# Order of TensorE in a graph-network layer: the turns of the next tile ahead of layer 3 of an older one

## The reference, cut to what matters

```python
# x (12500, 128), dst (200000,) sorted, edge_attr_48 (200000, 48)
h = jnp.maximum(_layernorm(x, axis=-1), 0.0)
agg_edge = jax.ops.segment_sum(edge_attr_48, dst, num_segments=12500)
collected = jnp.concatenate([h, agg_edge], axis=1)        # 128 + 48 columns
a = jax.nn.silu(collected @ W1 + b1)                      # 256
b = jax.nn.silu(a @ W2 + b2)                              # 256
return x + (h + b @ W3 + b3)                              # 128
```

## Time and profile before

| what | value |
|---|---|
| median of 3 runs | 288.13 us |
| lowest and highest | 286.89 and 288.31 us |
| the profiled execution | 288.73 us |
| its span in the trace | 287.0 us |
| PE, DVE, ACT, POOL busy | 96%, 84%, 77%, 47% of the span |
| mean granted TensorE clock | 0.994 of full speed |

### The profile page before, as it was taken

The page is one execution under the profiler, slowest core; times in us unless marked ns, Lnnn a source line. Parts: engine busy times, 40 slices in busy tenths (PEclk is TensorE's granted clock), DMA queues, the critical chain, the costliest instruction groups (busy, mean ns, idle before and its releaser), DMA issues.

```text
span 287.0 us, 11959 instructions
## 1 busy us (share of the span) xinstructions
PE 274.2 (96%) x4286; PEld 248.4 (87%) x4287; DVE 241.2 (84%) x583; ACT 220.3 (77%) x424; POOL 135.7 (47%) x248
## 2 busy tenths in 40 slices
PE   7868999999999999999999999999999999999994
PEld 3756988999999999999999999999999999999793
DVE  7887998889898898998998889989898888986551
ACT  8856778787886888778877788787976878779662
POOL 4275565454455445454555446454455445452200
PEclk9979999999999999999999999999999999999999
DMA  6998965865688457865687547955687567820112
GB/s 168 323 306 249 204 171 147 248 187 166 170 251 246 142 158 221 256 178 162 182 246 218 173 137 240 256 168 162 187 251 224 149 170 227 253 82 21 30 38 62
DMA packets 79309, 53.28 MB, mean 186 GB/s; under 512 B 2984, under 2 KB 78850, under 8 KB 79288
## 3 DMA queue, kind: packets, MB, share of 16 engines
q1 hardware_dynamic: 79288, 53.04, 63.6%
HBM read 46.29 MB, written 6.40 MB: 184 GB/s over the span
## 4 chain that ended last, share of the span: by engine, by line
PE 85%; DVE 5%; issue 3%; ACT 3%; POOL 2%; ACTq 0%; POOLq 0%; DVEq 0%
PE agg_ps L1109 21%; PE z L1176 15%; PE z L1157 7%; PE z L1161 7%; PE z L1158 7%; PE agg_ps L1112 4%; PE z L1137 4%; PE tp L1123 4%; PE z L1143 4%; PE z L1142 3%; PE z L1139 3%; PE z L1138 3%; DVE onehot L786 2%; PE agg_ps L1040 1%; POOL agg_carry L498 1%
## 5 line engine op out<-in xcount | busy, mean ns | idle before, releaser
L498 POOL TENSOR_TENSOR agg_carry<-staged,agg_carry 48x42 f32 x196 | 92.8, 474 | 77.1 <-ACT staged L554 46.3
L1109 PEld LDWEIGHTS agg_ps<-onehot,raw 128*48 128x48 f32 x1560 | 73.6, 126 | 12.1 <-issue 12.1
L1109 PE MATMUL agg_ps<-onehot,raw 128*48 128x42 f32 x1560 | 77.0, 216 | 3.5 <-DVE onehot L786 3.5
L786 DVE TENSOR_TENSOR onehot<-window,rel 128x1176 f32<-128x1176 f32 (+1 forms) x57 | 77.5, 1363 | 0.5 <-ACT rel L546 0.5
L1112 PE MATMUL agg_ps<-onehot,raw 128*48 128x42 f32 x1568 | 77.2, 216 | 0.0
L1112 PEld LDWEIGHTS agg_ps<-onehot,raw 128*48 128x48 f32 x1568 | 73.9, 127 | 0.0
L479 POOL TENSOR_TENSOR rstd<-vareps,minus_half 128x4 f32<-128x4 f32 (+1 forms) x28 | 37.7, 1346 | 46.4 <-DVE vareps L771 46.4
L1176 PE MATMUL z<-w,h 128*128 128x128 f32 x392 | 51.2, 282 | 1.5 <-ACT h L625 1.1
L625 ACT ACTIVATE h<-z,b2c 128x448 f32<-128x448 f32 (+1 forms) x56 | 35.4, 633 | 19.5 <-PE z L1161 17.1
L1176 PEld LDWEIGHTS z<-w,h 128*128 128x128 f32 x392 | 46.0, 191 | 3.2 <-ACT z L621 1.4
L941 DVE TENSOR_TENSOR h_lo<-h,h_hi 128x448 fp32r<-128x448 f32 (+1 forms) x56 | 34.8, 624 | 12.1 <-ACT h_hi L639 7.6
(11 more groups left out here) (129 smaller groups left out, 411.9 us busy)
## 6 DMA issues: line engine op xcount, KB each, us to landing
raw<-in_edge_attr_dram SPq DMA_DIRECT2D x55, 672.0 KB, 5.9
x_t<-in_x_dram SPq DMA_DIRECT2D x14, 256.0 KB, 6.1
out_dram<-out_t SPq DMA_DIRECT2D x13, 256.0 KB
out_dram<-out_t SPq DMA_DIRECT2D x14, 192.0 KB, 6.0
x_t<-in_x_dram SPq DMA_DIRECT2D x13, 192.0 KB, 6.2
dst_rows<-in_dst_dram SPq DMA_DIRECT2D x1, 512.0 KB
agg_carry<-agg_carry SPq DMA_DIRECT2D x1, 336.0 KB, 8.0
raw<-in_edge_attr_dram SPq DMA_DIRECT2D x1, 288.0 KB, 3.6
```

The source lines that it names most:

```text
L498: pool.tensor_tensor(into, staged[:, parity, n, :], into, ALU.add).then_inc(s_added, 1)
L786: return dve.tensor_tensor(onehot[:, slot, at * PER:n * PER, :], window[:, :].unsqueeze(1).broadcast_to([P, cols_n, WINDOW]), cols.unsquee ...
L1109: mm = pe.matmul(banks[0:ED, bass.ds(offsets[at - first], WINDOW)], edges, into, start=False, stop=True, skip_group_check=True, tile_posit ...
```

## The change

In TensorE's list for a step the turns of tile i and layer 3 of tile i-2 change places. No instruction is added or taken away, no wait has another count, and the lists of the other engines stay as they are.

```diff
@@ -1189,10 +1189,10 @@
                     layer1(i - 1, 1 - parity)
                 if has(i, -1, NB):
                     sum_tile(i + 1, 1 - parity, offsets)
+                if has(i, 0, NT):
+                    transposes(i, parity)
                 if has(i, 2, NT):
                     layer3(i - 2, parity)
-                if has(i, 0, NT):
-                    transposes(i, parity)
                 if isinstance(i, int) and i == 1:
                     pe.wait_ge(s_w_lo, 3)
                     pe.wait_ge(s_w_hi, 4)
```

## The result

| | before | changed |
|---|---|---|
| median | 288.22 us (4 runs, 286.89 to 288.87) | 301.50 us (4 runs, 301.37 to 302.02) |
| profiled execution, its span | 288.73, 287.0 us | 301.37, 299.7 us |
| PE busy, share of the span | 96% | 91% |

The ratio is 1.047 with a 95% interval of 1.043 to 1.050: slower, by 13.3 us. The prediction had the sign and the place right and the size too large: it said 305.4, and its range began at 302.5. One run of all that follow, of the kernel with the early rows in the new order, took 335.97 us at a mean granted clock of 0.756, and the median given for that kernel is that of its nine other runs.

A forecast was written before the change was run, and what follows sets the result against it. The prediction took TensorE's list to bound the kernel; new waits for ScalarE's rows (7.2 + 9.5 + 0.2 + 0.4 = 17.3 us) on 288.73 gave 306.0, less 0.6 for the median: 305.4 us, range 302.5 to 309.

The forecast's parts named there:

- What bounds it, and what the change adds: TensorE, 85% of the last-ending chain, would newly wait for ScalarE's rows in 25 steps, mostly 0.50 or 0.76 us.
- VectorE wasn't pushed: Rival: layer 3 ends later than worked out and delays VectorE and the next sums; some 3 us, 308.4 us, chance 0.04.
- From ScalarE's end to TensorE's start: Handover from finished rows to TensorE's turns, taken as 0.10 us per step, nothing added for filling up again.
- Step 3: One of 12 odd steps: rows 0.49 us late by subtraction, priced at 0.50 + 0.10 us like the others.
- Step 26: Its stall of 0.86 us was to absorb TensorE's 0.43 wait in step 27, so it costs 0.4 us.
- The base of the sum: The 17.3 us were added to the profiled execution of 288.73 us; 0.6 us came off for the runs' median.
- The clock rival: New gaps of 0.6 to 0.9 us drop TensorE's clock in 25 steps; 45 us on top, 350 us, chance 0.03.
- The issue gap: Rival: a fifth of the 12.1 us issue gap ahead of the sums comes back, 2.4 us; 303.0 us, chance 0.07.
- ScalarE did not get ahead: Rival: after one large stall later steps find the rows ready; 0.9 us in all, 289.0 us, chance 0.03.

The follow-up runs named there:

- early rows: ScalarE does the b3 fill and normalised rows ahead of layer 1's SiLU, against changed kernel and before: 289.92 us in the new order, 290.04 in the old.
- the wait alone: Against the kernel before, order kept, layer 3 also waits for the next tile's normalised rows: 304.98 us, ratio 1.061.
- warm start: More idle matmuls at the start, against before and the changed kernel: 287.46 us in the old order, 301.61 us in the new.

## Why the prediction was wrong in its size

**What bounds it, and what the change adds: right.** The rows came 0.49 and 0.77 us after TensorE was out of the sums (146.59 and 156.80, against 146.10 and 156.03, where the next matmul would have started 2.65 and 2.66 us behind the start of the sums, as before), as subtracted from the earlier trace rows; 25 steps have the wait; ScalarE's 0.38 before L635 stayed, so the wait came back in each step; VectorE wasn't pushed; the clock held. The runs with the wait alone and with early rows show that this is the whole loss.

**The term that was mis-sized: "From ScalarE's end to TensorE's start".** "I take 0.10, the middle of 0.05 and 0.14". It is 0.05 at the turns, and the new order gives that much back, a term that the sum had at nothing: from the first turn to layer 2 it is 148.74 - 146.65 = 2.09 us, where layer 3 and the turns took 143.83 - 141.69 = 2.14 before. The stop has no part in this. The kernel with early rows has the same 2.09 in the new order and never stops for rows, and the wait alone, which stops in the old order, takes 149.96 - 147.83 = 2.13. So a step costs its lag and nothing on top: 0.50 and 0.77 instead of 0.60 and 0.86. Over 11 odd and 11 even steps that is 11 x 0.10 + 11 x 0.09 = 2.1 us of the sum. I had two prices from two other places and averaged them; of my two cases the one with 0.14 had other waits at the same place.

**Step 3 cost next to nothing in this pair.** Before, layer 3 of step 3 has a stop of its own, behind its first matmul at 48.53 (PE, order of time):

```profile
49.35 1.83 PE L1176 MATMUL z<-w,h 128*128 128x128 f32 x15 [0.44 <-issue]
```

In the changed kernel the same stretch is

```profile
47.48 0.65 PE L1123 MATMUL tp<-ident,xn 128*128 128x128 f32 x3 [0.49 <-ACT xn L593]
47.98 1.95 PE L1176 MATMUL z<-w,h 128*128 128x128 f32 x16
```

The stop of 0.44 is no longer there; the wait for the rows lies over it. From step 3's sums to step 4's it is 10.05 us against 10.02 before. The kernel with the early rows in the new order has no wait there, and a stop of 0.76 us stands among its turns. How much of the stop the wait covers differs from run to run: in the repetition of the changed kernel a stop of 0.24 us stays behind the first turn, and the step takes 10.32. The earlier trace rows hold the mark of the stop (layer 3 of step 3 comes as x1 where step 25 has x16), and I didn't ask what it would do: 0.6 us of the sum. What makes the stop isn't shown.

**Step 26 cost 0.07, not 0.43.** TensorE's wait of 0.43 in step 27 went, as worked out; step 26 takes 282.08 - 272.20 = 9.88 us where it took 269.39 - 259.58 = 9.81. Of the stall of 0.77 that other even steps pay, 0.70 was free, and my price for that was the bracket's 0.43. The rows around it in the trace of before (PE, order of time):

```profile
267.38 0.37 PE L1143 MATMUL z<-agg_hilo,w1e_lo 112*128 112x448 f32 x1
...
268.49 0.36 PE L1138 MATMUL z<-hT_hi,w1x_lo 128*128 128x448 f32 x1
```

A bracket counts from the end of the matmul before, here 267.38 + 0.37 = 267.75. In flow a matmul of this form starts 0.20 behind the start of the one before, at 267.58, so the one at 268.17 is 0.59 late. The next follows at 268.49, 0.32 later instead of 0.20, and that is another 0.12: together 0.71. Against the sum it is 0.4 us.

These make 17.3 - 2.1 - 0.6 - 0.4 = 14.2 us; 14.45 is measured. The 11 odd and 11 even steps cost 0.51 and 0.78 on average, a little more than steps 13 and 14, and that is most of the rest.

**The base of the sum.** "17.3 us on the profiled execution of 288.73 us": that execution has a start that the changed kernel's did not share. Its clock (PE alone; length, busy, granted clock, DMA share, GB/s), first before, then changed:

```profile
18.00:21.00 3.00, 2.43 (x62) 0.50 1.07 316
21.00:22.51 1.51, 1.51 (x58) 0.87 0.94 262
```

```profile
18.00:20.63 2.63, 2.63 (x112) 1.00 1.06 334
```

Batch 1's sums take from 18.57 to 22.51, most of it at half clock, and from 17.91 to 20.63 at full. That is the 1.76 us, 1.22 of it in the sums and the rest in when they could begin. The half clock of the earlier trace rows was in my rows, as an argument for a rival; that an execution without it is shorter was not in the base. Across runs it is worth less than in this pair, since the clock varies in both kernels: the medians are 13.3 apart, and runs with a full clock in both twins of the warm start 13.9. The runs at full clock of the two kernels themselves, four of before and three of the changed one, lie 301.37 - 287.15 = 14.2 us apart. So of the 4.0 us between my 17.3 and the 13.3, 2.9 are terms of the sum, and 1.1 is left for the start, which by these runs was slower in most runs of before; how its share divides between the clock and the moment at which its data arrive stays open.

**The rivals.** The clock rival is out for this kernel: 24 gaps of 0.47 to 0.77 us leave the granted clock at 1.00, and the eight runs of the changed kernel have means of 0.988 to 1.00. The Trainium skill's rule on short idle times between groups of matmuls (TensorE: Matmul & The Clock Gate, "A second HAM failure mode: psum-queue depth-cycling") doesn't show in this kernel at one gap in 10 us. The issue gap was not won back: each step still has its 0.31 ahead of the sums, and the row's total went from 12.1 to 11.3 by the first steps. ScalarE did not get ahead.

## What to carry to other kernels

Before a block that waits is moved ahead of one that doesn't, subtract: when does its operand come, and when does the engine get there? If the operand's maker is itself started by this engine a fixed time before, the difference is paid in every pass, and an order that looks idle (layer 3 between the sums and the turns) is the cover of somebody's latency. Price the handover by the row nearest in form to the new wait. Price a stop from start to start and not by its bracket. And ask of each stop that the trace of before already has whether the new wait will lie over it.

## What the runs showed of the hardware

A TensorE that has stopped for ScalarE's rows starts 0.05 us after their recorded end at the turns, but 0.06 or 0.24 at layer 3 with the wait ahead of its own two waits, and 0.14 or 0.15 with the wait behind them. What in TensorE's list makes these differences wasn't settled. The expectation's register operation in even steps is in no view of the profile, and at most a part of the difference could be its.

At the start of the kernel TensorE can work for a while at half clock (1.2 instead of 2.4 GHz): 33 of the 37 runs of before have a mean granted clock of 0.987 to 0.994. In the trace of before, behind idle times of 0.69, 1.12 and 1.64 us, it is from 18.57 us on, for some 3 us. Idle time alone doesn't decide it: the kernel with early rows in the new order has an idle time of 1.64 us at the same place and a mean granted clock of 0.998, and the changed kernel has one of 1.55 us at 10.20 and 1.00. Two other traces, with means of 0.987 and 0.988, have 0.50 from about 11 to 18 us and from about 10 to 17 us. Later, in full work, idle times of up to 0.94 us in 25 steps (the wait alone) left the clock at 1.00.
